# The combine stage of a soft mixture-of-experts layer rewritten as a stream of chunks, with row maxima broadcast from DRAM

## What is computed

```python
logits = jnp.einsum('bnd,esd->bnes', x, se)
dispatch = jax.nn.softmax(logits, axis=1)
combine = jax.nn.softmax(logits.reshape(x.shape[0], x.shape[1], -1), axis=-1)
slots = jnp.einsum('bnd,bnes->besd', x, dispatch)
...
eout = eout.reshape(eout.shape[0], -1, eout.shape[-1])
return jnp.einsum('bns,bso->bno', combine, eout)
```

## Time and profile before

| | us |
|---|---|
| median of 3 runs | 2116.95 (2116.89 to 2117.19) |
| span of the profiled execution | 2117.7 |
| TensorE busy in it | 1879.6 (89%) |
| DVE busy | 1510.7 (71%) |
| ACT busy | 1017.6 (48%) |
| POOL busy | 679.2 (32%) |
| first combine stage, first instruction to last result | 714.4 to 928.7 |
| second combine stage | from 1898.7 on, to the last result at 2113.5 |

### The profile page before, as it was taken

How to read it: one execution, slowest core, us unless ns; L and a number is a source line. 1 busy time by engine, 2 the same in 40 slices (tenths; PEclk the granted TensorE clock), 3 DMA queues, 4 the chain that set the end, 5 groups by cost and what they waited for, 6 DMA issues and landing times. The chain is left out here.

```text
span 2117.7 us, 35275 instructions
## 1 busy us (share of the span) xinstructions
PE 1879.6 (89%) x11782; PEld 1661.7 (78%) x11782; DVE 1510.7 (71%) x3055; ACT 1017.6 (48%) x2057; POOL 679.2 (32%) x619
## 2 busy tenths in 40 slices
PE   1799999988699899968999968999999859989999
PEld 1678787877699699968999846878778649978998
DVE  5777777763588899944555467767776348889997
ACT  0044445456455577734343302444354645547775
POOL 1422221100366455512222133212220007745553
PEclk9999999999899899988999979999999989998999
DMA  2353233320355466731212135332332115536774
GB/s 80 145 194 128 92 139 129 120 100 21 125 193 184 154 239 241 258 122 45 75 59 71 43 128 202 134 140 99 119 130 100 70 60 193 176 132 225 262 261 163
DMA packets 96785, 293.78 MB, mean 139 GB/s; under 512 B 7712, under 2 KB 47520, under 8 KB 84384
## 3 DMA queue, kind: packets, MB, share of 16 engines
q1 hardware_dynamic: 96672, 292.39, 38.9%
HBM read 183.31 MB, written 109.05 MB: 138 GB/s over the span
## 5 line engine op out<-in xcount | busy, mean ns | idle before, releaser
L76 POOL TENSOR_TENSOR pool_carrier<-minus_half 128x1 f32<-128x1 f32 x108 | 23.4, 217 | 668.9 <-DVE f2r_mv L352 289.4
L366 DVE TENSOR_SCALAR_CACHE_REDUCE f2r_lt<-f2r_ps_l,slot_shift 128x512 f32<-128x512 f32 x128 | 95.5, 747 | 87.3 <-PE f2r_ps_l L570 69.1
L366 DVE TENSOR_SCALAR_CACHE_REDUCE f1r_lt<-f1r_ps_l,slot_shift 128x512 f32<-128x512 f32 x128 | 95.5, 747 | 86.7 <-PE f1r_ps_l L570 68.6
L1122 PE MATMUL f2c_ps_y<-f2c_eo,f2c_e_hi 128*128 128x258 f32 (+1 forms) x512 | 151.0, 300 | 3.4 <-ACT f2c_e_hi L1078 3.2
L1122 PE MATMUL f1c_ps_y<-f1c_eo,f1c_e_hi 128*128 128x258 f32 (+1 forms) x512 | 151.1, 300 | 2.8 <-ACT f1c_e_hi L1078 2.7
L1123 PE MATMUL f1c_ps_y<-f1c_eo,f1c_e_hi 128*128 128x256 f32 (+1 forms) x512 | 143.8, 286 | 0.0
L1123 PE MATMUL f2c_ps_y<-f2c_eo,f2c_e_hi 128*128 128x256 f32 (+1 forms) x512 | 143.7, 286 | 0.0
L1133 PE MATMUL f1c_ps_y<-f1c_eo,f1c_e_lo 128*128 128x258 f32 (+1 forms) x512 | 135.7, 285 | 0.0
L1133 PE MATMUL f2c_ps_y<-f2c_eo,f2c_e_lo 128*128 128x258 f32 (+1 forms) x512 | 135.7, 285 | 0.0
L518 ACT ACTIVATE f2r_e_hi<-f2r_ps_t 128x512 fp32r<-128x512 f32 x128 | 69.7, 594 | 101.3 <-PE f2r_ps_t L583 101.2
L518 ACT ACTIVATE f1r_e_hi<-f1r_ps_t 128x512 fp32r<-128x512 f32 x128 | 69.7, 594 | 101.3 <-PE f1r_ps_t L583 101.2
(11 more groups left out here) (289 smaller groups left out, 6666.4 us busy)
## 6 DMA issues: line engine op xcount, KB each, us to landing
logits<-f1r_lt SPq DMA_DIRECT2D x16, 2048.0 KB, 7.3
f1c_lt<-logits SPq DMA_DIRECT2D x32, 1024.0 KB, 7.4
logits<-f2r_lt SPq DMA_DIRECT2D x16, 2048.0 KB, 7.3
f2c_lt<-logits SPq DMA_DIRECT2D x32, 1024.0 KB, 7.2
f1r_xin<-in_L_attn_x SPq DMA_DIRECT2D x16, 512.0 KB, 5.2
normalized<-f1r_xin SPq DMA_DIRECT2D x16, 512.0 KB, 2.6
f1r_xback<-normalized SPq DMA_DIRECT2D x16, 512.0 KB, 8.0
f1e_raw_g<-in_L_ffn_Wg SPq DMA_DIRECT2D x16, 512.0 KB, 4.1
```

The source lines that it names most:

```text
L76: pool.tensor_tensor(c["pool_carrier"][:, col:col + 1], c["minus_half"][:, 0:1], c["minus_half"][:, 0:1], ALU.add)
L366: dve.tensor_scalar(lt[:, g, sc, :], ps_l[sc % 2][:, :], c["slot_shift"][:, sc:sc + 1], None, ALU.add, ALU.max, accum_out=gmax[:, sc, g:g ...
L1122: pe.matmul(ps_y[t][:, 0:LO], e_hi[par][:, sc, tile], eo[:, bpar, sc, 0:LO], start=sc == 0, stop=False)
```

## The change

The stage is rewritten as a stream of chunks.

- The row maxima are transposed by TensorE at the start of `expert_stage`, copied to SBUF by ACT and stored in DRAM by SP. In the combine stage SP loads each group's 512 maxima onto all 128 partitions (`load_max_rows`). The diagonals and `spread_max` go, and the shift adds two SBUF operands, `lt` and `max_rows`.
- `e_hi` and `e_lo` have one buffer instead of two. ACT waits for TensorE's `chunk_used` (chunks 0 to 4) or `mixed` (5 to 7) of the group before.
- BY_POOL is (1, 3, 5, 7). For the four chunks of DVE the exponential goes to one of two PSUM banks `ps_e` and is read from there for the high and the low part; for those of POOL it stays in `lt`.
- TensorE goes through chunks 0 to 5 with the tiles inside, a chunk's low part one step behind its high part; what is left (high parts 6 and 7, low parts 5 to 7, 7 matmuls for each tile) is done tile by tile.
- DVE, ACT and POOL work on the group that TensorE works on. DVE's shift is AHEAD = 3 chunks in front of the step, its low part one chunk, ACT's exponential one chunk. The finishes of tiles 0, 1 and 2 stand at the end of DVE's steps 6 and 7, that of tile 3 at the start of the next group.
- `slot_out_hi` is done after chunk 3 and chunk 7; on POOL `slot_out_lo` keeps its place behind the first and the second low part of a group.
- The loads for group i+2 wait for POOL's low parts (and the maxima for the last shift) of group i.

```diff
+def expert_stage(nc, c, tag, prm, slots, eout, neg_row_max, max_rows_dram):
...
+        max_rows = al.sb("max_rows", [B * NG * GT, P])
+        ps_m = al.ps("ps_m", [P, BANK])
+        max_tr, max_out, max_stored = (al.sem(n) for n in ("max_tr", "max_out", "max_stored"))
...
             emit(0, True)
             emit(1, False)
+            sp.wait_ge(max_out, 1)
+            sp.dma_start(max_rows_dram.rearrange("i (t p) -> (i t) p", p=P), max_rows[:, :]).then_inc(max_stored, DMA)
...
+            sp.wait_ge(max_stored, DMA)
...
             weights_hi(0, 0, 0, True)
+            act.wait_ge(max_tr, 1)
+            act.activation(max_rows[:, :], ps_m[0:B * NG * GT, 0:P], ACT.Copy).then_inc(max_out, 1)
...
+            pe.transpose(ps_m[0:B * NG * GT, 0:P], neg_row_max[:, :, :, :].rearrange("p b g t -> p (b g t)"),
+                         c["ident"][:, :]).then_inc(max_tr, 1)
             hidden(0, 0, True)
...
+def combine_stage(nc, c, tag, x_in, x_out, logits_dram, max_rows_dram, eout):
...
-    BY_POOL = (1, 4, 6)
+    BY_POOL = (1, 3, 5, 7)
     BY_DVE = tuple(sc for sc in range(NSC) if sc not in BY_POOL)
+    TAIL = 5
+    AHEAD = 3
...
-        e_hi = [al.sb(f"e_hi{i}", [P, NSC, GN], F32R) for i in range(2)]
-        e_lo = [al.sb(f"e_lo{i}", [P, NSC, GN], F32R) for i in range(2)]
+        e_hi, e_lo = al.sb("e_hi", [P, NSC, GN], F32R), al.sb("e_lo", [P, NSC, GN], F32R)
...
-        diag = al.sb("diag", [P, GT, P])
+        max_rows = [al.sb(f"max_rows{i}", [P, GN]) for i in range(2)]
...
-        ps_r = [al.ps(f"ps_r{i}", [P, BANK]) for i in range(2)]
+        ps_e = [al.ps(f"ps_e{i}", [P, BANK]) for i in range(2)]
...
+            def load_logits(n, par, h):
+                half = slice(h * NSC // 2, (h + 1) * NSC // 2)
+                sp.dma_start(lt[par][:, half, :], logits_dram[n][:, half, :]).then_inc(lt_loaded[par][h], DMA)
+
+            def load_max_rows(n, par):
+                sp.dma_start(max_rows[par][:, :], max_rows_dram[n:n + 1, :].to_broadcast([P, GN]) if isinstance(n, int) else
+                             max_rows_dram[bass.ds(n, 1), :].to_broadcast([P, GN])).then_inc(rows_loaded[par], DMA)
...
+            load_logits(0, 0, 0)
+            load_max_rows(0, 0)
+            load_logits(0, 0, 1)
+            load_max_rows(1, 1)
             load_x(0, 0)
-            load_logits(1, 1)
+            load_logits(1, 1, 0)
+            load_logits(1, 1, 1)
             load_x(1, 1)
...
-                    if exists(b, g, 2):
-
-                        sp.wait_ge(mixed, GT * i + 1)
-                        load_logits(i + 2, g % 2)
                     if known(b, g) >= 1:
                         store(i - 1, (g + 1) % 2)
                         if exists(b, g, 1):
                             load_x(i + 1, (g + 1) % 2)
+                    if exists(b, g, 2):
+
+                        for h in range(2):
+                            sp.wait_ge(lo_by_pool, len(BY_POOL) * i + (h + 1) * len(BY_POOL) // 2)
+                            load_logits(i + 2, g % 2, h)
+                        sp.wait_ge(shifted, NSC * (i + 1))
+                        load_max_rows(i + 2, g % 2)
...
-            def max_diagonals(b, g, n):
-
-                if n is not None and (not isinstance(n, int) or n > 0):
-                    pool.wait_ge(max_mm, n)
-                pool.tensor_tensor(diag[:, :, :], c["ident"][:, :].unsqueeze(1).to_broadcast([P, GT, P]),
-                                   neg_row_max[:, b, g, :].unsqueeze(2).to_broadcast([P, GT, P]),
-                                   ALU.mult).then_inc(diag_done, 1)
...
-                pool.tensor_tensor(e_lo[par][:, sc, :], lt[par][:, sc, :], rd(e_hi[par][:, sc, :]),
+                pool.tensor_tensor(e_lo[:, sc, :], lt[par][:, sc, :], rd(e_hi[:, sc, :]),
...
-            max_diagonals(0, 0, 0)
             pool.memset(rd(eo[:, :, :, D:LO]), 2.0).then_inc(twos_done, 1)
-            max_diagonals(0, 1, 1)
-            for sc in BY_POOL:
-                lo_part(0, 0, sc)
             def emit(b):
                 for g in range(NG):
                     i = b * NG + g
-                    if exists(b, g, 2):
-                        max_diagonals(b + (g + 2) // NG, (g + 2) % NG, i + 2)
                     for m, sc in enumerate(BY_POOL):
-                        if exists(b, g, 1):
-                            lo_part(i + 1, (g + 1) % 2, sc)
+                        lo_part(i, g % 2, sc)
                         if exists(b, 0, NG) and m < NSC // NG:
                             slot_out_lo(b + 1, (b + 1) % 2, NSC // NG * g + m)
...
                 if sc == 0:
-                    dve.wait_ge(max_mm, n + 1)
+                    dve.wait_ge(rows_loaded[par], DMA * (n // 2 + 1))
                 if sc % (NSC // 2) == 0:
                     dve.wait_ge(lt_loaded[par][sc // (NSC // 2)], DMA * (n // 2 + 1))
-                dve.tensor_tensor(lt[par][:, sc, :], lt[par][:, sc, :], ps_r[par][:, :], ALU.add).then_inc(shifted, 1)
+                dve.tensor_tensor(lt[par][:, sc, :], lt[par][:, sc, :], max_rows[par][:, :], ALU.add).then_inc(shifted, 1)
             def lo_part(n, par, sc):
+
                 dve.wait_ge(hi_done, NSC * n + sc + 1)
-                dve.tensor_tensor(e_lo[par][:, sc, :], lt[par][:, sc, :], rd(e_hi[par][:, sc, :]),
+                dve.tensor_tensor(e_lo[:, sc, :], ps_e[BY_DVE.index(sc) % 2][:, :], rd(e_hi[:, sc, :]),
                                   ALU.subtract).then_inc(lo_by_dve, 1)
...
-            def prepare(n, par, before, done):
-
-
-                order = ("s0", "s1", "s2", "F3", "l0", "s3", "s4", "s5", "l2", "s6", "f0", "l3", "s7", "f1", "l5", "f2", "l7")
...
-
+            for sc in range(AHEAD):
+                shift(0, 0, sc)
             for sc in range(NSC):
                 dve.wait_ge(eo_hi_done, sc + 1)
                 dve.tensor_tensor(eo[:, 0, sc, LO:W], eout[:, 0, sc, :], rd(eo[:, 0, sc, 0:D]), ALU.subtract)\
                    .then_inc(eo_lo_done, 1)
-            prepare(0, 0, lambda: None, lambda t: None)
+            lo_part(0, 0, 0)
             def emit(b):
                 for g in range(NG):
                     i = b * NG + g
                     n = known(b, g)
-                    before = (lambda: finish(i - 1, (g + 1) % 2, GT - 1, n < 3)) if n >= 1 else (lambda: None)
-                    done = lambda t: finish(i, g % 2, t, n < 2)
-                    if exists(b, g, 1):
-                        prepare(i + 1, (g + 1) % 2, before, done)
-                    else:
-                        before()
-                        for t in range(GT):
-                            done(t)
+                    for sc in range(NSC):
+                        if sc == 0 and n >= 1:
+                            finish(i - 1, (g + 1) % 2, GT - 1, n < 3)
+                        if sc == NSC - 1:
+                            finish(i, g % 2, 1, n < 2)
+                        nxt = (sc + 1) // NSC
+                        if exists(b, g, nxt) and (sc + 1) % NSC in BY_DVE:
+                            lo_part(i + nxt, (g + nxt) % 2, (sc + 1) % NSC)
+                        nxt = (sc + AHEAD) // NSC
+                        if exists(b, g, nxt):
+                            shift(i + nxt, (g + nxt) % 2, (sc + AHEAD) % NSC)
+                        if sc == NSC - 2:
+                            finish(i, g % 2, 0, n < 2)
+                        if sc == NSC - 1:
+                            finish(i, g % 2, 2, n < 2)
             batches(dve, emit)
+            finish(LAST, 1, GT - 1, False)
...
-            def exponential(n, par, sc):
+            def exponential(n, par, sc, first):
+
                 act.wait_ge(shifted, NSC * n + sc + 1)
-                act.activation(lt[par][:, sc, :], lt[par][:, sc, :], ACT.Exp).then_inc(exp_done, 1)
+                if sc in BY_DVE:
+                    k = BY_DVE.index(sc)
+                    if not (first and k < 2):
+                        act.wait_ge(lo_by_dve, len(BY_DVE) * n + k - 1)
+                    act.activation(ps_e[k % 2][:, :], lt[par][:, sc, :], ACT.Exp).then_inc(exp_done, 1)
+                else:
+                    act.activation(lt[par][:, sc, :], lt[par][:, sc, :], ACT.Exp).then_inc(exp_done, 1)
             def hi_part(n, par, sc, first):
-                if sc == 0 and not first:
-                    act.wait_ge(mixed, GT * (n - 1))
+
                 act.wait_ge(exp_done, NSC * n + sc + 1)
-                act.activation(e_hi[par][:, sc, :], lt[par][:, sc, :], ACT.Copy).then_inc(hi_done, 1)
-
-            def prepare(n, par, first):
-                for sc in range(NSC + 1):
-                    if sc < NSC:
-                        exponential(n, par, sc)
-                    if sc >= 1:
-                        hi_part(n, par, sc - 1, first)
+                if not first:
+                    if sc < TAIL:
+                        act.wait_ge(chunk_used, TAIL * (n - 1) + sc + 1)
+                    else:
```

(67 more changed lines are left out.)

49 lines of the change are left out of this document (12 added, 37 removed).

## The result

The changed kernel takes 2365.09 us, median of 4 runs (2362.67 to 2367.94), beside 2116.92 for the kernel before on the same chip: 1.1177 times as long, 95% interval 1.1161 to 1.1193. The forecast was 2320 with a range of 2250 to 2385. The first combine stage takes 336.1 us, from its first eo hi part at 713.66 to its last finish at 1049.8, and the second 339.9; before they took 214.3 and 214.9. That is 121.8 and 125.0 us, 246.8 together; the two profiled spans lie 243.1 apart. The rest of the kernel, 3.7 us shorter in this profile, has moved by no more than the runs scatter.

A forecast was written before the change was run, and what follows sets the result against it. TensorE was taken to bound the kernel before, DVE having next to no slack. Start, turns, pieces and end made a combine stage 315.7 us against 214.3; twice the difference, 202.7, on the 2117.7 span gave 2320, range 2250 to 2385.

The forecast's parts named there:

- rival 4: Combine stage stays bound by TensorE and chunks flow, gaining 31 us and 6 us at two starts: 2075; chance 0.04.
- Part 1: Removing spread_max frees TensorE 0.98 us a group, 31 us in all, a gain only if TensorE sets the pace.
- Part 2, the ring: Mid-group, DVE's shift and low part and four ACT operations wait in a circle: 3.54 us per two chunks, TensorE wanting 2.86.
- rival 2: Only the ring counts, POOL's queue not holding up its last low parts: groups 17.1, stage 282, kernel 2253; chance 0.12.
- Part 3, the turn: Between groups, POOL's slot-output lo part holds up its last low parts: 7.90 us in batches 0 to 2, 5.65 in batch 3.
- rival 1: TensorE's clock falls in the turn, tail matmuls taking twice 3.4 us: 36 to 72 us, 2356 to 2392; chance 0.17.
- The piece after the turn: Finishes of tiles 2 and 3 stand before the new group's chunk-3 shift; up to its chunk-4 shift, 4.34 us.
- Part 4: DVE's shift with two SBUF operands contends with POOL: excess 0 to 0.98 us each, only chunk 6's hit, by about 0.3.
- Rival 3: DVE sets the pace through shift contention, excess 0.30 to 0.36 each, ACT far ahead: 2108 to 2124; chance 0.07.
- Sum of a stage: Start, turns, pieces between and last group add to 315.7 us per combine stage against 214.3 before.
- the piece from S(4) to S(6): Between the shifts of chunks 4 and 6, POOL's late low part adds to the ring: 4.13 us.
- Part 5, the rest: Maxima steps in expert_stage cost 0 to 1 us a stage; broadcast loads delay the first group's first shift about 0.6 us.

The follow-up runs named there:

- e9: Kernel before, its order kept, but maxima broadcast by DMA and copied by ACT into PSUM for the shift, no spread_max: 2126.11 us, ratio 1.0034.
- e5: Kernel before, its order kept, but maxima broadcast by DMA, shift adding two SBUF operands, no spread_max: 2156.34 us, ratio 1.0193.
- e10: e8 with finishes of tiles 1 to 3 in a row and ACT's copy of the maxima a group earlier: 2101.53 us, ratio 0.9930.
- e11: Changed kernel with AHEAD = 5, POOL's slot-output lo parts behind its low parts, finishes in one piece, shift from SBUF: 2140.78 us, ratio 1.0116.
- e2: Changed kernel with AHEAD = 4 instead of 3, nothing else: 2194.81 us, ratio 1.0379.
- e1: Changed kernel with POOL doing a group's slot-output lo parts behind its four low parts: 2273.0 us, ratio 1.0740.
- e6: Changed kernel with 20 unread TensorE matmuls in each group's turn, before the waits for POOL's last two low parts: 2343.14 us, ratio 1.1070.
- e3_ahead5_pool: Changed kernel with AHEAD = 5 and POOL's slot-output lo parts behind its low parts: 2120.88 us, ratio 1.0026.
- e8: Changed kernel with AHEAD = 5, POOL's slot-output lo parts behind its low parts, broadcast maxima copied by ACT to PSUM: 2120.08 us, ratio 1.0011.
- e4: Changed kernel with maxima spread by diagonals and spread_max into PSUM, as before, and no expert-stage steps: 2338.91 us, ratio 1.1055.
- e7: Changed kernel with AHEAD = 5, POOL's slot-output lo parts behind its low parts, maxima spread into PSUM by spread_max: 2114.36 us, ratio 0.9996.

## Why the prediction was right, and where it was off

**Bound of the kernel before.** Incomplete. TensorE was busy all the time, but DVE, noted as having next to no slack, was as much a bound (e9, e5). The prediction's 12.38 is the distance of TensorE's groups while it still had room: up to 845.15 its `spread_max` came every 12.32 to 12.38 us, but DVE's finishes every 12.60 from the first group on, and then TensorE came near that pace too, 12.48 to 12.61 (timeline of TensorE, kernel before):
```profile
857.67 1.12 PE L1111 MATMUL f1c_ps_r<-f1c_diag,ones 128*128 128x512 f32 x2
...
870.28 1.12 PE L1111 MATMUL f1c_ps_r<-f1c_diag,ones 128*128 128x512 f32 x2
```
The oversight touched only rival 4 and the gain named in Part 1: the 31 us could not have come by themselves. A stream that flows needed DVE relieved as well (e10 against e11).

**Part 2, the ring.** Right in its links and its size: 3.51 to 3.60 us against 3.54, ACT's wait for a shift once in two chunks, DVE's for a hi part of up to 2.0 us. e2 shows that the lead sets it. TensorE's own time for two chunks is a slip, 24 x 0.12 being 2.88 and not 2.86; nothing hangs on it. A stage with the ring and without the turn's block takes 292 us (e1); rival 2 had 282.

**Part 3, the turn.** Right in its mechanism: with the slot-output lo part out of the way 92 us go (e1), and in batch 3, which has none, all four pieces and the group of 17.1 were met within 0.1. Rival 2, by which POOL's queue does no harm, is refuted. In batches 0 to 2 the turn was too short by 0.98 us (8.88 against 7.90). Two terms were mis-sized. One is the clock: 28 matmuls of the tail were taken at full speed; rival 1 had the fall, but as another course with its own sum. With the clock held the turn is 7.89 to 8.42, mean 8.08 (e6), so the clock is 0.80 of the 0.98. The rest is small: in the turn shown L(7) ended 5.25 after S(0') against 4.82, as the slot-output lo part started 0.6 after its input instead of 0.07.

**The piece after the turn.** Forecast 4.34, mean 4.79: in four of the 12 it is 5.6, in the others 4.3 to 4.5. In the group shown F(3) is late by the low clock (831.13, idle 0.52 before it), so that S(3') starts behind POOL's L(1') and takes 1.37. With the clock held (e6) none of these pieces is over 4.44 and their mean is 4.32, as forecast. Part 4 had only S(6) hit.

**Part 4, the SBUF operand.** The mechanism was right and its frequency too low. The Trainium skill (SBUF — State Buffer, "SBUF: two separate sides") has a DVE operation with two SBUF inputs and a GpSimd operation that reads SBUF exclude each other. The rows agree: S(3') at 831.74 ends at 833.11, 0.55 after POOL's operation that started first at 831.27 (832.56), and DVE's lo parts, now from PSUM, keep to 689 ns. Rival 3 did not come about, since ACT was never ahead; once it is, as in e3_ahead5_pool, e5 and e11, its mechanism appears: an excess of 0.26 to 0.39 a shift answers to its 0.30 to 0.36. In e3_ahead5_pool the wait for the finishes is a limit of the same 12.53 beside it (e8).

**Sum of a stage.** 336.1 against 315.7. By the ACT timeline of the first stage: start +0.9 (the broadcast of the first maxima lands 0.8 later than was taken), 12 turns +11.7, the pieces after them +5.4, the next +2.1, the ring +0.4, batch 3 and the end nothing; together +20.5. Over both stages the loss above the forecast is 45 us. By the pieces of e6 about 34 of it is the clock, which the forecast had at nothing. The remaining 11 are, by the same pieces, 2 in the starts, about 4 in the turns without the clock (the late slot-output parts), 4 in the piece from S(4) to S(6), where the two shifts took 0.50 longer (838.79, 1.78 for two, against 1.28) and 0.3 was allowed, and 1 in the ring.

**Part 5, the rest.** Right: the expert stages have not grown, and e4, which drops their steps, is faster than the changed kernel by 26.2 us, of which its two combine stages make 25.5.

**Rivals.** The outcome is the forecast's turn and ring with rival 1's clock in it, inside the 2356 to 2392 that rival 1 gave; of its price, 36 to 72 us, e6 shows some 34. By the prediction's own signs, a clock at 0.5 in the turns spoke for rival 1, which had a chance of 0.17, and not for the forecast. The range covered the result because it took in most of rival 1. The argument that the gaps were "just below what fell" in the earlier trace rows took each gap for itself. Between the two gaps TensorE did a few matmuls only, and the clock fell right after the second.

## What to carry to other kernels

Before an order that works groups ahead is made into a stream, write down each engine's order, follow the waits round from an engine to itself, and compare the sum with the bound's time for as many chunks: here 3.5 us against 2.9, which one more step of lead mended for 170 us. Look in each in-order queue for a step whose input comes late and which stands ahead of urgent ones (92 us here for two lines in another place). And take an operation off the busiest engine only after asking whether a second one is as busy; here a gain came only with the maxima in PSUM, the finishes early and ACT's copy a group ahead (e10), and it was 14 us of the 31 hoped for.

## What the runs showed of the hardware

The granted clock fell to 0.50 within a stretch of gaps in which TensorE still did a few matmuls (at 822.10 and 824.78, gaps of 1.66 and 2.17 us before them), whereas a single gap of 1.3 us had left it at 1.00. After TensorE was fully busy again at 826 it came back between 831 and 832. Twenty unread matmuls in the same gaps kept it at 1.00 (e6), which was worth about 34 us, and cost 12 in batch 3, where the lo parts came early.

The exclusion between DVE and POOL works in both directions. This lo part of POOL in the kernel after took 1.79 us instead of 1.29 while DVE did a shift:
```profile
853.84 1.79 POOL L985 TENSOR_TENSOR f1c_e_lo<-f1c_lt,f1c_e_hi 128x512 fp32r<-128x512 f32 x1 [5.33 <-ACT f1c_e_hi L1089]
```
The same wait thus makes a shift or a lo part longer, whichever comes second. With the PSUM operand the shift showed no such wait: 677 to 680 ns in every kernel that had it (e4, e7, e8, e9, e10).
